# The second step of every routed group moves 256 rows always

## What is computed

```
h = tok_mlp(codebook[x])                               # 256 -> 1024 -> 256, tanh gelu
h = h + gru(layernorm(h))                              # two layers of a gated scan
n = layernorm(h)
shared = (gelu(n @ w1s) * (n @ w2s)) @ w3s             # 256 -> 1024 -> 256, every token
idx = argmax(n @ Wg)                                   # one of 8 experts for each token
routed = (gelu(n @ W1[idx]) * (n @ W2[idx])) @ W3[idx]
out = h + shared + routed
```

## Time and profile before

| | |
|---|---|
| median of 3 runs | 482.52 us (482.36 to 483.57) |
| the profiled execution's own time | 484.04 us |
| its span, first to last instruction | 482.3 us |
| TensorE busy | 474.3 us, 98% of the span |
| VectorE, ScalarE, GpSimd busy | 330.8, 246.9, 78.4 us |
| granted TensorE clock | full in all slices |

### The profile page before, as it was taken

How to read it: one execution, slowest core, us unless ns; L and a number is a source line. 1 busy time by engine, 2 the same in 40 slices (tenths; PEclk the granted TensorE clock), 3 DMA queues, 4 the chain that set the end, 5 groups by cost and what they waited for, 6 DMA issues and landing times.

```text
span 482.3 us, 8608 instructions
## 1 busy us (share of the span) xinstructions
PE 474.3 (98%) x3052; PEld 424.1 (88%) x3053; DVE 330.8 (69%) x559; ACT 246.9 (51%) x376; POOL 78.4 (16%) x92
## 2 busy tenths in 40 slices
PE   8999999999999999999999999999999999999997
PEld 7998888889888888888889988889999998999887
DVE  3659668678686887767554687537876696678464
ACT  3766774575653464343334656236545463645321
POOL 4431031011011010102360001100101011011460
PEclk9999999999999999999999999999999999999999
DMA  5952121001210002100444467304553566341192
GB/s 158 335 178 86 34 76 56 33 23 55 61 63 1 1 0 101 76 0 23 152 159 83 126 237 258 132 23 167 192 197 121 185 239 207 120 141 72 55 335 90
DMA packets 26425, 56.07 MB, mean 116 GB/s; under 512 B 7248, under 2 KB 19664, under 8 KB 22416
## 3 DMA queue, kind: packets, MB, share of 16 engines
q1 hardware_dynamic: 19312, 43.45, 26.4%
q0 software_dynamic: 2976, 8.14, 5.1%
q10 hardware_dynamic: 4096, 3.93, 2.8%
HBM read 43.16 MB, written 12.35 MB: 115 GB/s over the span
## 4 chain that ended last, share of the span: by engine, by line
PE 93%; DVE 3%; issue 1%; DMA 1%; ACT 1%; DVEq 0%; POOLq 0%
PE ps L285 25%; PE ps L287 25%; PE ps L286 25%; PE ps L816 6%; PE ps L818 3%; PE ps L846 2%; PE ps L848 1%; DMA q<-codebook_in,idx_sb 1%; PE ps L622 1%; PE ps L704 1%; PE ps L669 1%; PE ps L657 1%; PE ps L837 1%; DVE stats L1321 1%; PE ps L682 0%
## 5 line engine op out<-in xcount | busy, mean ns | idle before, releaser
L285 PE MATMUL ps<-xW,w_slots 128*128 128x256 f32 (+1 forms) x256 | 72.6, 284 | 0.9 <-issue 0.9
L286 PE MATMUL ps<-xW,w_slots 128*128 128x256 f32 (+1 forms) x256 | 71.6, 280 | 0.0
L287 PE MATMUL ps<-xW,w_slots 128*128 128x256 f32 (+1 forms) x256 | 71.6, 280 | 0.0
L1256 DVE TENSOR_TENSOR hT<-ps,hT 128x512 fp32r<-128x512 f32 x64 | 43.9, 686 | 35.6 <-ACT hT L995 15.7
L491 POOL DMA_INDIRECT y_tokens<-y_rows,to_rows x30 | 31.8, 1062 | 184.1 <-DVE y_rows L1660 174.4
L285 PEld LDWEIGHTS ps<-xW,w_slots 128*128 128x128 f32 x256 | 48.9, 191 | 2.0 <-issue 1.5
L286 PEld LDWEIGHTS ps<-xW,w_slots 128*128 128x128 f32 x256 | 49.0, 191 | 0.0
L287 PEld LDWEIGHTS ps<-xW,w_slots 128*128 128x128 f32 x256 | 48.9, 191 | 0.0
L816 PE MATMUL ps<-w_slots,hW 128*128 128x512 f32 x128 | 46.6, 401 | 0.0
L995 ACT ACTIVATE hT<-ps 128x512 fp32r<-128x512 f32 x32 | 19.1, 598 | 52.7 <-DVE ps L1262 48.0
L1133 ACT ACTIVATE w_slots<-stage 128x2048 fp32r<-128x2048 f32 x24 | 45.8, 1910 | 0.0
(11 more groups left out here) (213 smaller groups left out, 1282.8 us busy)
## 6 DMA issues: line engine op xcount, KB each, us to landing
stage<-ew_in SPq DMA_DIRECT2D x24, 1024.0 KB, 4.8
x_sorted<-zero_row SPq DMA_DIRECT2D x32, 128.5 KB
stage<-w1s_in SPq DMA_DIRECT2D x2, 1024.0 KB, 8.4
fetched<-y_tokens SPq DMA_DIRECT2D x4, 512.0 KB
x_pair<-x_sorted ACTq DMA_DIRECT2D x7, 256.0 KB, 2.7
x_one<-x_sorted ACTq DMA_DIRECT2D x7, 256.0 KB
out_rows<-fetched SPq DMA_DIRECT2D x3, 512.0 KB
first_stage<-tok_w_in SPq DMA_DIRECT2D x1, 1024.0 KB
```

Source lines behind the costliest of these rows:

```text
L285: pe.matmul(dst, lhs_hi, rhs_hi, start=start, stop=False, skip_group_check=shares_bank)
L286: pe.matmul(dst, lhs_hi, rhs_lo, start=False, stop=False, skip_group_check=shares_bank)
L287: return pe.matmul(dst, lhs_lo, rhs_hi, start=False, stop=stop, skip_group_check=shares_bank)
L1256: dve.tensor_tensor(hT[:, c % RING, 1, :], ps[:, bank, :], f32(hT[:, c % RING, 0, :]), ALU.subtract).then_inc(h_lo, 1)
```

## The change

Step 1 calls `window_up` itself, without the branch, so that it moves 256 rows in every group. Steps 2 and 3 are left as they are.

```diff
@@ -906,7 +906,7 @@
                                 with pe.If((count - j) > 0):
                                     next_single(e, s, m, j, odd)
                     single_turn(last_of(pe, e), 0)
-                window_up_of(more, e, 1, odd)
+                window_up(e, 1, odd)
                 with pe.If(count > 0):
                     single_turn(last_of(pe, e), 1)
                 pe.wait_ge(w_lo, e * PAIRS + 1)
```

## The result

| | before | changed |
|---|---|---|
| median of 6 runs each | 482.44 us | 485.12 us |
| lowest to highest | 481.85 to 483.57 | 484.31 to 486.33 |
| profiled execution: own time, span | 484.04, 482.3 us | 484.53, 482.8 us |

The ratio is 1.0054, with an interval of 1.0036 to 1.0072: +2.6 us. The forecast was 483.3 us, no change that can be told, in a range that ended at 484.6.

The account below looks back on a forecast made before the run. The prediction took TensorE, busy 98% of the span, to bound the kernel. Its terms, +0.84 + 0 + 0 us on the 482.52 us median, gave 483.3 us, with an 8-in-10 range of 481.9 to 484.6.

Parts of the forecast that it names:

- Part 1: Step 1 of the four few groups: 256 columns instead of 192, 0.21 us for each step, +0.84 us.
- The rival that columns are paid in full: Step 1's 96 narrow matmuls: 64 more columns cost 30 ns each, 2.9 us, total 485.4 us; chance 3%.
- Part 2: Step 1 on TensorE's sequencer: 16 fewer branches in the 8 groups, already hidden by queued matmuls, 0 us.
- Part 3: Group 1's idles from late code: 51 fewer instructions per copy shift block borders, changes cancel, 0 us.
- the term that was to shrink: Group 1's 1.11 us idle before the next window's transposes: block needed some 0.4 to 1 us later, shorter idle.
- the growing term: Group 1's 0.73 us idle before step 1, behind the jump over the singles: probably longer, by about the other's shrinking.
- a block comes later than now: Late code at group 1's step 1 or in group 0 or 2: +1.2 us over 0.84, 484.6 us; chance 14%.

Follow-up runs that it names:

- before again: The kernel before, unedited, timed and traced a second time; 482.9 us in the median, ratio 0.9997.
- the changed kernel again: The changed kernel, unedited, timed and traced a second time against the kernel before; 485.47 us, ratio 1.0048.

## Why the prediction was wrong

**Part 1, the columns: right in kind, mis-sized.** The sum had 0.84 us, the measured term is 0.5. A wide step is 0.20 us longer (2.95 us in group 2 against 2.75), but the matmuls behind the narrow steps start a little closer in the changed kernel, so groups 2 and 6 are each 0.15 us longer, group 7 0.18, and group 0 not at all, because a wide step there covers the 0.16 us of idle that "narrow" left before step 3. That is four times 0.16, less 0.16. I had taken steps by themselves and not a group's length. The rival that columns are paid in full, 2.9 us, is out, and with it the 2.6 us that the prediction worked out by the gap rule of the Trainium skill's "TensorE: Matmul & The Clock Gate" ("Back-to-back issue gap").

**Part 2, the branch: 0, right.** Groups 3 and 5 last 17.81 us before and after. The count was off: 12 executed branches have gone, not 16.

**Part 3 is the step that failed**, at "with one term that probably grows and one that probably shrinks by about the same, I take **0**". Three things were wrong in it. First, the term that was to shrink can't be set against the growing one in full: the idle before the transposes is in the first trace of the kernel before, but in neither of the two others with its places (18.50 and 19.10 us in group 1, not 20.38). The idles were read from an execution of 484.04 us, while the sum was put on the median, 482.52. In the first two traces the terms do cancel, 20.38 against 20.45 us, which looks like the forecast of 20.4; that is luck, as against the trace of 18.50 us each term is 1.9 us, and neither was sized so. Second, the size of the growing term: the request moves by 51 places and the idle grows from 0.44 to 2.38 us; the text said that the border would "move toward or past" the jump, and priced a late block at +1.2 us from the idles in view. Against the trace without the second idle, group 1 gained 1.95 us. Third, nothing in the sum stood for what an idle of 2.4 us does to the clock: about 1.5 us more in about half of the runs.

Put together, from the trace of before again to that of the changed kernel, over the whole routed part:

```profile
265.78:442.92 177.14, 176.00 (x1257) 163.83 (x1256) 126.66 (x159) 95.04 (x121) 19.18 (x18) 1.00 0.47 164
```

```profile
265.19:445.14 179.95, 176.82 (x1257) 164.63 (x1255) 126.89 (x159) 95.20 (x121) 19.14 (x18) 1.00 0.47 162
```

2.81 us: 1.95 in group 1, 0.35 of late code in group 7, 0.5 of columns. The medians are 2.7 us apart. That the two agree is in part chance: the medians hold in addition the half clock in about half of the changed kernel's runs, and on the other side executions of the kernel before in which its second idle does come.

The mechanism itself had been named: late blocks of code, at the jump over the singles, in group 1, with groups 3 to 5 untouched. The rival "a block comes later than now" was the true case, with a price of 1.2 us where 1.95 plus the clock belonged. In the runs the jump waits for 3.4 us, the matmul comes 2.4 to 2.9 us behind the packet's start (3.3 once), and 51 places move the idle between 0.2 and 2.4 us in group 7 and between 0.4 or 0.6 and 2.4 in group 1. The Trainium skill's "Runtime: NRT & Kernel Launch" ("Instruction fetch mechanics") warns of just this taken branch out of the loaded window, which the traces bear out.

Shown are: that the places decide (five kernels with nothing but unexecuted places added, and the change in group 0 alone), that the jump is needed (the two runs without it), that in group 1 the branch instruction is what waits, and the share of the columns. Inferred, from their timing against this branch, is that the packets belong to TensorE's program; and that in code without a jump a block is asked for when the one before it is entered. Open stay the exact borders (group 7's idles with 64 and group 0's with 192 places came out otherwise than I had placed them), what the 2.5 us between packet and matmul consist of, why the second idle of the kernel before comes and goes, and why the clock falls after some of the idles of over 2 us and not after others.

Four kernels beat the kernel before: the changed one with 128 places (0.9961) and the one before with 64 (0.9985), which work with any input, though their placing was tried with this one alone; and the two without the singles code in odd groups (0.9970 and 0.9956), which are only right for inputs in which these groups have no singles.

## What to carry to other kernels

Where a program branches over code that it meets for the first time, where this code lies is a cost of its own: removing 51 instructions from each copy cost some 2 us beyond the columns, and adding 128 that are never executed gained 4. Before a small edit to such a program is judged, hold the places fixed (let the dead branch do the new work) and then move them alone. And before an idle of a single trace goes into a sum, take a second trace, above all when the profiled execution isn't near the median.

## What the runs showed of the hardware

An idle of 2.1 to 2.5 us on a TensorE that had been busy throughout was followed, in some executions and not in others, by 3.2 to 3.4 us at a granted clock of 0.50. The traces hold eight such idles. The clock fell behind five (of 2.40, 2.37, 2.32, 2.13 and 2.53 us, in groups 1, 7, 0, 0 and 1) and not behind three (2.38, 2.12 and 2.30 us, in groups 1, 1 and 7), so their length doesn't decide. It cost 1.5 us beyond the idle, and shows in a run without a trace as a mean clock of 0.996. Of 102 runs of the kernel before, whose traces have idles of 0.4 to 1.1 us, none showed it; 6 of 13 of the changed kernel's did.

A taken jump to code that the program met for the first time held the sequencer for up to 3.6 us in group 1 (the changed kernel again) and 3.8 in group 7 (with 51 places), and for 0.21 us where the same code ran again in groups 3 and 5.

From one matmul's start to the next, with a weight load in front of each, it is 111 ns at 192 columns and 120 at 256, but 230 ns at 512 (24 matmuls from 361.12 to 366.63 us, the singles of group 4): the 64 columns from 192 to 256 are nearly free here, the next 256 are not.
